# Second attention: beta's addition on VectorE, scatter tails set by halves of a round

## The chip, the core and the metric

The kernel runs on one core of a Trainium2 chip. The metric is the device time of one execution in microseconds (us). PE is TensorE, DVE VectorE, ACT ScalarE, POOL GpSimd, SP SyncE. TensorE's clock has two levels, 1.2 and 2.4 GHz; the profile gives the granted clock as a share of the full one.

## The reference

Four layers act on x, 4096 tokens (64 sequences of 64) of 256 floats, all in float32; each adds its result to x.

```python
x = x + xattn0(layernorm(x), ctx)       # attention over the channel axis, 8 heads
x = x + ffn0(layernorm(x))              # 16 experts, the best 2 per token, and a shared expert
x = x + xattn1(layernorm(x), ctx)       # below
x = x + ffn1(layernorm(x))              # 32 experts, the best 4 per token

# the end of xattn1: ctx_h are the heads' results
delta = rs * (ctx_h @ Wo.T + bo)
delta = (delta - mean(delta)) / sqrt(var(delta) + 1e-5) * ln_gamma + ln_beta

# ffn1, as ffn0 in its routing
logits = x @ gate_w.T + gate_b
top, idx = top_k(logits, 4); weight = softmax(top)
y = sum over the 4 of weight * expert[idx](x)
```

## The kernel before

All 32 tiles of x (128 tokens x 256) stay in SBUF. The stages follow each other, each written as one list of steps per engine; each engine runs its list in order and waits on semaphores. Eight groups of four tiles (`GT = 4`, `NG = 8`) are routed. Stages: the first attention (to about 785 us), the shared expert with the first routing (788 to 905), the first experts (to 1060), the second attention with the second routing (1060 to 1440), the second experts (to 1710), and a last stage that sums and stores.

**Routing.** For a group, VectorE picks the best K experts of each token (`choose`), PE counts ranks (`make_ranks`), VectorE turns them into row numbers in a DRAM tensor `rows_in` (`place_rows`, semaphore `slots_ready`) and writes weights (`weigh`, or ScalarE's sigmoids in the shared expert). GpSimd then sends the group's rows in K rounds (`scatter`): round k writes the normalised row of each token to its k-th expert's place, with four indirect DMAs, one per tile. A row is 272 floats: 256 of the token and a tail of 16, whose first two are `DEST` (where the expert's result for this token and k belongs in `by_token`) and `WEIGHT`. GpSimd copies these two into the tail before each round, which needs the DMAs of the group's round before to have read the row. `tails_set` counts the rounds whose tails are set. K is 2 in the first routing, 4 in the second, 32 rounds there.

**Second attention.** Step r of each engine's list works on several tiles at once (j = r % 4, g = r // 4). VectorE, in order: `choose` for group g-2 (j = 0), the norm of group g+2 (j = 3), `clip` of r+1 (L1862), statistics, `place_rows` and `weigh` for g-2 (j = 1), `residual` of r-2 (L1897, L1900), `normalise` of r (L1869, L1872), `delta_statistics` of r-1 (L1880 to L1889). Residual: `scaled = (delta - mean) * gamma`, then `x = scaled * rstd + xb`, where `xb = x + beta` comes from GpSimd (`add_beta`, L1975). PE in step r: `values`, `scores` of r+1 (L1650), transposes, `context_transposes` of r-1 (L1668; waits for VectorE's heads and delta), keys or queries, `outputs` of r (L1679), `projection` of r-1 (L1687), logits of g-1 (L1071, j = 3), ranks of g-2 (j = 0). GpSimd in step r: `delta_deviation` of r-2 (L1981, the power -1/2 that the residual needs), `add_beta` of r-1, a round of scatters from r = 10 on, the power for a group's norm (L1456). Before r = 4 or so it also adds the first experts' results to x (`add_parts`, L1964 and L1967). The 32 rounds go one per step in a fixed list; after the first 22 come, by group and k, (5,2), (6,0), (5,3), (6,1), (7,0), (6,2), (7,1), (6,3), (7,2), (7,3). The last six need the last group's routing or follow it.

**SP's queue at the end of this stage.** 16 pieces of 0.5 MB of the next experts' weights `w_gu` go into a region the attention used (L1609). Each waits for a value of `tails_set`, so that they are spread over the last rounds:

```python
for n, (into, source) in enumerate(later):
    sp.wait_ge(rt.tails_set, len(in_order) + 1 + n * (len(rounds) - len(in_order) - 2) // len(later))
    sp.dma_start(into, source).then_inc(later_written, 16)
```

With 22 in order and 32 in all, piece n waits for 23 + n // 2. Behind them on SP, `table_pads` writes a block of 128 zero rows behind each expert's last row, 16 on SP's queue and 16 on ScalarE's, four row numbers loaded (L722) and then four DMAs (L726), and then the experts' block loads begin (L863). The experts read each block's `DEST` and `WEIGHT` with ScalarE and store the weighted results with indirect DMAs on GpSimd.

## Time and profile before

| | |
|---|---|
| median of 3 runs | 1776.12 us (1773.91 to 1784.85) |
| profiled execution | 1775.95 us, of which 1774.0 between first and last instruction |
| mean granted TensorE clock | 0.944 |
| busy, share of the span | PE 86%, DVE 75%, ACT 62%, POOL 62% |
| DMA moved | 167.66 MB, mean 95 GB/s |

Busy shares are means over stages with different limits. A row of the order of time reads: start, duration, engine, line, operation, output and input, shape, and in brackets how long the engine stood idle before it and what ended that. In the chain of waits each row is the start and length of a piece of the chain that ended last. "remote" is a semaphore whose setter the profile did not identify. L numbers are lines of the kernel before.

### The profile page before, as it was taken

What the parts mean: (1) busy time and instruction counts of PE and PEld (TensorE: products, weight loads), DVE (VectorE), ACT (ScalarE), POOL (GpSimd) and SP (SyncE); (2) the same over time, 40 slices, a digit from 0 to 9 for tenths busy, and PEclk for the clock granted to TensorE, in tenths of its full rate; (3) what the DMA queues carried; (4) which work ended last, traced back from release to release, by engine and by line L of the source; (5) the groups of instructions that cost most, each with busy time, mean ns of one, the idle gap of its engine ahead of it and who ended that gap; (6) DMA issues with size and microseconds to landing.
All of it is one profiled execution on the core that took longest, in us unless ns stands there. A gap on an engine that the chain in (4) does not pass through costs nothing.

```text
span 1774.0 us, 43982 instructions
## 1 busy us (share of the span) xinstructions
PE 1533.0 (86%) x14968; PEld 1236.6 (70%) x14968; DVE 1332.5 (75%) x2901; ACT 1094.1 (62%) x3516; POOL 1093.0 (62%) x1111
## 2 busy tenths in 40 slices
PE   6999999999999999989967755998895179999966
PEld 5888888888888888866646642565564179998955
DVE  6889899899999989876634344798886248887876
ACT  5888888888888888843335433656551056666610
POOL 4767667676666667647635554647776636666642
PEclk9999999999999999989989986999995589999988
DMA  8400000000000000022255424112213855554456
GB/s 230 128 20 20 20 20 20 20 20 20 12 19 20 20 20 20 8 97 84 79 176 155 151 80 161 49 38 94 83 71 113 311 167 165 162 158 150 125 200 275
DMA packets 103082, 167.66 MB, mean 95 GB/s; under 512 B 20224, under 2 KB 75981, under 8 KB 102481
## 3 DMA queue, kind: packets, MB, share of 16 engines
q1 hardware_dynamic: 73984, 103.46, 19.1%
q0 software_dynamic: 22272, 56.15, 8.6%
q10 hardware_dynamic: 6608, 5.25, 1.0%
q8 instruction: 124, 2.03, 0.5%
q14 instruction: 94, 0.76, 0.2%
HBM read 95.31 MB, written 75.76 MB: 96 GB/s over the span
## 4 chain that ended last, share of the span: by engine, by line
PE 68%; DVE 11%; issue 9%; POOL 3%; another core or an unknown queue 3%; ACT 2%; ACTq 1%; DMA 1%; SPq 1%; DVEq 0%; POOLq 0%
PE layers_banks L323 13%; PE layers_banks L294 13%; PE layers_banks L309 9%; PE layers_banks L890 9%; PE layers_banks L901 5%; PE layers_banks L1269 3%; PE layers_banks L277 3%; PE layers_banks L283 3%; PE layers_banks L878 2%; DVE weights L1862 2%; PE layers_banks L1282 1%; PE layers_banks L2152 1%; POOL l_rows_in L1179 1%; PE layers_banks L1071 1%
## 5 line engine op out<-in xcount | busy, mean ns | idle before, releaser
L468 POOL TENSOR_TENSOR w_down<-w_down,layers_arena 128x1024 f32<-128x1024 f32 x256 | 483.5, 1894 | 230.3 <-DVE layers_arena L424 229.3
L389 ACT ACTIVATE w_down<-layers_banks,layers_arena 128x256 f32<-128x256 f32 x1024 | 468.7, 498 | 2.8 <-DVE layers_arena L418 2.8
L1010 POOL DMA_INDIRECT l_by_token<-layers_arena x240 | 245.0, 1021 | 192.3 <-issue 104.2
L429 DVE COPY w_down<-layers_banks 128x1024 f32<-128x1024 f32 x256 | 312.2, 1220 | 40.4 <-PE layers_banks L309 36.2
L418 DVE TENSOR_REDUCE layers_arena<-layers_banks 128x4 f32<-128x1024 f32 x256 | 309.4, 1209 | 29.4 <-PE layers_banks L294 29.3
L294 PE MATMUL layers_banks<-layers_arena 64*128 64x256 f32 x2048 | 277.9, 383 | 3.7 <-ACT w_down L389 2.2
L323 PE MATMUL layers_banks<-w_down,layers_arena 128*64 128x256 f32 x2048 | 249.4, 385 | 1.7 <-DVE w_down L429 1.3
L389 ACT ACTIVATION_READ_ACCUMULATOR w_down<-layers_banks,layers_arena 128x1 f32 x1024 | 238.0, 232 | 0.0
L890 PE MATMUL layers_banks<-layers_arena 128*128 128x128 f32 x1600 | 204.1, 280 | 34.3 <-ACT layers_arena L933 30.7
L1179 POOL DMA_INDIRECT l_rows_in<-layers_arena,l_routing_group_slots x192 | 190.3, 991 | 57.7 <-issue 44.7
L309 PEld LDWEIGHTS layers_banks<-ident,w_down 64*128 64x128 f32 x4096 | 168.4, 138 | 77.5 <-issue 71.6
L890 PEld LDWEIGHTS layers_banks<-layers_arena 128*128 128x128 f32 x1600 | 192.3, 195 | 40.4 <-issue 40.0
L294 PEld LDWEIGHTS layers_banks<-layers_arena 64*128 64x128 f32 x2048 | 208.7, 188 | 6.0 <-issue 5.5
L309 PE MATMUL layers_banks<-ident,w_down 64*128 64x64 f32 x4096 | 178.7, 224 | 17.4 <-DVE w_down L429 3.4
L323 PEld LDWEIGHTS layers_banks<-w_down,layers_arena 128*64 128x64 f32 x2048 | 142.1, 136 | 61.5 <-DVE w_down L429 1.5
L986 DVE TENSOR_SCALAR layers_arena<-layers_banks,layers_arena 128x256 f32<-128x256 f32 x240 | 104.5, 477 | 75.5 <-PE layers_banks L901 41.0
L924 ACT ACTIVATE layers_arena<-layers_banks 128x512 f32<-128x512 f32 x120 | 70.5, 587 | 92.8 <-PE layers_banks L878 78.2
L353 ACT ACTIVATE layers_arena<-layers_banks 128x512 f32<-128x512 f32 x128 | 75.8, 592 | 82.0 <-PE layers_banks L283 82.0
L933 ACT ACTIVATE layers_arena<-weights 128x512 f32 (+1 forms) x240 | 119.6, 547 | 3.7 <-issue 3.7
L957 DVE TENSOR_SCALAR layers_arena<-layers_banks,l_block_bias 128x128 f32<-128x128 f32 x160 | 48.8, 346 | 87.1 <-PE layers_banks L890 84.7
L878 PE MATMUL layers_banks<-ident,layers_arena 128*128 128x128 f32 x480 | 75.4, 281 | 44.0 <-DMA layers_arena<-l_rows_in 44.0
L878 PEld LDWEIGHTS layers_banks<-ident,layers_arena 128*128 128x128 f32 x480 | 61.9, 146 | 57.0 <-issue 44.1
(227 smaller groups left out, 2552.3 us busy)
## 6 DMA issues: line engine op xcount, KB each, us to landing
layers_arena<-l_rows_in SPq DMA_DIRECT2D x240, 136.0 KB
weights<-l_by_token SPq DMA_DIRECT2D x32, 512.0 KB, 9.7
layers_arena<-in_ctx SPq DMA_DIRECT2D x64, 128.0 KB, 2.7
layers_arena<-l_by_token SPq DMA_DIRECT2D x32, 256.0 KB, 2.7
weights<-in_w_gu SPq DMA_DIRECT2D x16, 512.0 KB
l_rows_in<-zeros SPq DMA_DIRECT2D x1, 4352.0 KB
x_sb<-in_x SPq DMA_DIRECT2D x32, 128.0 KB, 2.5
w_down<-in_w_down SPq DMA_DIRECT2D x1, 4096.0 KB
```

The source lines that it names most:

```text
L294: last = nc.tensor.matmul(ps_s[:, b, 2 * h + qt, :], q_sb[half, p % 2, b, qt * P:(qt + 1) * P], ctx_d[half, p // TILE % 2, b, :], start=Tr ...
L309: last = nc.tensor.transpose(ps_t[:, d, kt, c * S:(c + 1) * S], prob[half, n % 4, c, kt * P:(kt + 1) * P], ident[half, half])
L323: last = nc.tensor.matmul(ps_qo[b * S:(b + 1) * S, 0, 0:A_N], vb[:, p // TILE % 2, kt, b, head * S:(head + 1) * S], prob_t[:, p % 2, b, kt ...
L389: last = nc.scalar.activation(prob[:, n % 4, c, :], ps_s[:, n % 2, c, :], ACT.Exp, bias=negmax[:, n % 2, c:c + 1], accum_out=sums[:, n % 2 ...
L418: nc.vector.tensor_reduce(negmax[:, n % 2, :], ps_s[:, n % 2, :, :], AX.X, ALU.max, negate=True).then_inc(max_ready, 1)
L429: nc.vector.tensor_copy(prob_t[:, n // 2 % 2, n % 2, :, :, :].rearrange("p k c (d s) -> p d (k c) s", d=2), ps_t[:, :, :, :].rearrange("p ...
L468: nc.gpsimd.tensor_tensor(prob[:, n % 4, :, :], prob[:, n % 4, :, :], rsum[:, n % 2, :].unsqueeze(2).to_broadcast([P, 4, A_N]), ALU.mult). ...
L878: last = nc.tensor.transpose(ps_x[:, q % 2, b, kt, :], rows[:, q % BODY, b, kt * P:(kt + 1) * P], sb["ident"][:, :])
L890: last = nc.tensor.matmul(ps_gu[:, q % 2, u, b, :], w_now[:, q % 2, b, kt, u * P:(u + 1) * P], rows_t[:, q % 2, b, kt, :], start=(kt == 0) ...
L933: last = nc.scalar.activation(w_now[:, r % 2, b, :, :].rearrange("p k n -> p (k n)"), w_gu[:, bass.ds(e[b], 1), :, :].rearrange("p a k n - ...
L1010: pool.indirect_dma_start(m.by_token, bass.IndirectOffsetOnAxis(ap=place, axis=0), outs[:, r % OUTS, b, :], None, bounds_check=T * m.K - 1 ...
L1179: pool.indirect_dma_start(m.rows_in, bass.IndirectOffsetOnAxis(ap=self.slots[:, slot, n:n + 1], axis=0), xn[:, j, :], None).then_inc(self. ...
```

## The change

`add_beta` leaves GpSimd; VectorE does the same addition at the start of `residual`, ahead of the waits for the power and for `scaled`, and the wait for `xb_ready` now stands before the last instruction. `place` (integers) and `weight` (floats) become one float tensor `tails` with the two side by side; one copy sets both numbers. A round is cut into halves of two tiles, each with its copy, its wait on `tails_set`, its two DMAs and a semaphore of its own, `scattered[slot][half]`, so the copy for a half waits only for the DMAs of the same half of the round before. `tails_set` counts halves, and the values on which SP's weight pieces wait are rewritten. ScalarE turns `DEST` into an integer when it copies it in the experts.

```diff
-        self.place = sbt("_place", [P, NG, K, GT], I32)
-        self.weight = sbt("_weight", [P, NG, K, GT], F32)
+        self.tails = sbt("_tails", [P, NG, K, GT, 2], F32)
...
                 nc.scalar.activation(dest[:, q % TAILS, :].bitcast(I32),
-                                     rows[:, q % BODY, :, DEST].bitcast(I32), ACT.Copy)
+                                     rows[:, q % BODY, :, DEST], ACT.Copy)
...
-        self.scattered = [ph.sem(f"scattered{n}") for n in range(Routing.RING)]
+        self.scattered = [[ph.sem(f"scattered{n}_{half}") for half in range(2)] for n in range(Routing.RING)]
...
     def scatter(self, pool, it, q, xn, k, turn, done):
-        sent = 16 * GT
+        sent = 16 * (GT // 2)
         slot, lap = (it * 2 + q) % self.RING, (it * 2 + q) // self.RING
         if k == 0:
             done(pool, self.slots_ready, it, q)
             done(pool, self.weights_ready, it, q)
-        else:
-            pool.wait_ge(self.scattered[slot], lap * sent * m.K + sent * k)
-        nc.gpsimd.tensor_copy(xn[:, :, DEST].bitcast(I32), m.place[:, it * 2 + q, k, :])
-        nc.gpsimd.tensor_copy(xn[:, :, WEIGHT], m.weight[:, it * 2 + q, k, :]).then_inc(self.tails_set, 1)
-        pool.wait_ge(self.tails_set, turn + 1)
-        for j in range(GT):
-            n = j * m.K + k
-            pool.indirect_dma_start(m.rows_in, bass.IndirectOffsetOnAxis(ap=self.slots[:, slot, n:n + 1], axis=0),
-                                    xn[:, j, :], None).then_inc(self.scattered[slot], 16)
+        for half in range(2):
+            tiles = slice(half * GT // 2, (half + 1) * GT // 2)
+            if k > 0:
+                pool.wait_ge(self.scattered[slot][half], lap * sent * m.K + sent * k)
+            nc.gpsimd.tensor_copy(xn[:, tiles, DEST:WEIGHT + 1], m.tails[:, it * 2 + q, k, tiles, :]).then_inc(self.tails_set, 1)
+            pool.wait_ge(self.tails_set, 2 * turn + half + 1)
+            for j in range(half * GT // 2, (half + 1) * GT // 2):
+                n = j * m.K + k
+                pool.indirect_dma_start(m.rows_in, bass.IndirectOffsetOnAxis(ap=self.slots[:, slot, n:n + 1], axis=0),
+                                        xn[:, j, :], None).then_inc(self.scattered[slot][half], 16)
...
-            sp.wait_ge(rt.tails_set, len(in_order) + 1 + n * (len(rounds) - len(in_order) - 2) // len(later))
+            sp.wait_ge(rt.tails_set, 2 * len(in_order) + 2 + 2 * n * (len(rounds) - len(in_order) - 2) // len(later))
...
         def residual(it, r):
+            tdone(dve, x_ready, it, r - 1)
+            nc.vector.tensor_tensor(xb[:, r % 2, :], tile, w["beta"][:, :], ALU.add).then_inc(xb_ready, 1)
             tdone(dve, rstd_d_ready, it, r)
-            tdone(dve, xb_ready, it, r)
-            tdone(dve, x_ready, it, r - 1)
             nc.vector.scalar_tensor_tensor(out=scaled[:, :], ...).then_inc(scaled_ready, 1)
             tdone(dve, scaled_ready, it, r)
+            tdone(dve, xb_ready, it, r)
             nc.vector.scalar_tensor_tensor(out=tile, ...).then_inc(x_ready, 1)
...
-        def add_beta(it, r):
-            tdone(pool, scaled_ready, it, r - 2)
-            tdone(pool, x_ready, it, r - 2)
-            nc.gpsimd.tensor_tensor(xb[:, r % 2, :], x_sb[...], w["beta"][:, :], ALU.add).then_inc(xb_ready, 1)
...
-            if texists(it, r - 1):
-                add_beta(it, r - 1)
```

`mark_sent` waits for both halves; `weigh`, the sigmoids of the shared expert and the last stage write or read `tails[..., 1]` instead of `weight`; the iotas of the places and of the zero rows' `DEST` make floats.

## Rows read from the trace of the kernel before

**Rows 1.** Busy time by stretch (us; instructions), PEclk, DMA share, GB/s
```profile
core 0: us, PE busy (x) PEld busy (x) DVE busy (x) ACT busy (x) POOL busy (x), PEclk, DMA share, GB/s
788.00:905.00 117.00, 107.99 (x543) 70.86 (x541) 71.40 (x325) 40.95 (x70) 74.20 (x102) 0.99 0.27 101
1226.00:1259.00 33.00, 29.73 (x301) 19.80 (x301) 28.95 (x96) 19.45 (x33) 24.61 (x34) 1.00 0.26 85
1390.00:1415.00 25.00, 1.43 (x4) 1.03 (x4) 2.25 (x8) 0.00 (x0) 18.89 (x27) 0.50 1.04 383
```

**Rows 2.** Chain of waits, end of the shared expert: start, us, what
```profile
906.16 1.77 DMA l_rows_in<-zeros
```

**Rows 3.** Order of time, GpSimd then VectorE, end of part A
```profile
1141.08 0.55 POOL L1981 TENSOR_TENSOR layers_arena<-layers_arena,minus_half 128x1 f32<-128x1 f32 x1
1141.60 0.73 POOL L1975 TENSOR_TENSOR layers_arena<-x_sb,w_beta 128x256 f32<-128x256 f32 x1
...
1141.67 0.94 DVE L1897 SCALAR_TENSOR_TENSOR layers_arena<-layers_arena,w_gamma 128x256 f32<-128x256 f32 x1 [2.81 <-POOL layers_arena L1981]
```

**Rows 4.** Waits of VectorE, 1143 to 1349 us: total, times, longest
```profile
DVE weights L1862 <- remote: 4.9, 3, 2.4
DVE layers_arena L1082 <- remote: 3.6, 2, 1.8
DVE weights L1862 <- PE layers_banks L1650: 1.4, 1, 1.4
...
DVE layers_arena L1465 <- POOL layers_arena L1456: 0.3, 2, 0.2
```

**Rows 5.** Order of time, GpSimd, last rounds of scatters
```profile
1387.27 0.19 POOL L1174 COPY layers_arena<-l_place 128x4 int32<-128x4 int32 x1 [1.70 <-DVE l_weight L1126]
...
1416.89 0.19 POOL L1174 COPY layers_arena<-l_place 128x4 int32<-128x4 int32 x1 [2.58 <-DMA l_rows_in<-layers_arena,l_routing_group_slots]
...
1417.48 0.98 POOL L1179 DMA_INDIRECT l_rows_in<-layers_arena,l_routing_group_slots  x1 [0.28 <-POOL layers_arena L1175]
1418.77 0.96 POOL L1179 DMA_INDIRECT l_rows_in<-layers_arena,l_routing_group_slots  x1 [0.30 <-issue]
...
1421.29 0.96 POOL L1179 DMA_INDIRECT l_rows_in<-layers_arena,l_routing_group_slots  x1 [0.30 <-issue]
```

**Rows 6.** Chain of waits over SP's queue, end of the attention
```profile
1404.28 0.93 SPq L1609
...
1407.07 0.36 SPq L726
...
1408.72 0.69 SPq L726
...
1418.96 0.33 SPq L726
...
1419.48 0.33 SPq L726
...
1423.26 1.93 DMA l_rows_in<-zeros
```

**Rows 7.** GpSimd's groups by line, 1050 to 1440 us
```profile
L1975 POOL TENSOR_TENSOR layers_arena<-x_sb,w_beta 128x256 f32<-128x256 f32 x32 | 23.9, 747 | 0.0
...
L1174 POOL COPY layers_arena<-l_place 128x4 int32<-128x4 int32 x32 | 8.4, 261 | 14.1 <-DMA l_rows_in<-layers_arena,l_routing_group_slots 12.3 <-DVE l_weight L1126 1.7
```

**Rows 8.** VectorE's groups by line, 1143 to 1349 us
```profile
L1897 DVE SCALAR_TENSOR_TENSOR layers_arena<-layers_arena,w_gamma 128x256 f32<-128x256 f32 x25 | 12.2, 486 | 0.3 <-issue 0.3
```

**Rows 9.** Order of time, VectorE, inside part B
```profile
1221.80 0.47 DVE L1897 SCALAR_TENSOR_TENSOR layers_arena<-layers_arena,w_gamma 128x256 f32<-128x256 f32 x1
...
1226.65 0.29 DVE L1082 TENSOR_TENSOR layers_arena<-layers_banks,w_gate_b 128x128 f32<-128x128 f32 x1 [1.76 <-remote]
```

**Rows 10.** Order of time, VectorE, start of the attention
```profile
1068.55 0.42 DVE L1848 TENSOR_TENSOR x_sb<-x_sb,layers_arena 128x256 f32<-128x256 f32 x1
1068.89 0.42 DVE L1846 TENSOR_TENSOR layers_arena<-layers_arena 128x256 f32<-128x256 f32 x1
```

**Rows 11.** Chain of waits in part B, PE's last piece
```profile
1320.47 1.72 PE layers_banks L1071 x16
```

More of the change, by code:

```diff
@@ L1125, in weigh @@
         dve.sem_inc(self.passed, 1)
-        nc.vector.tensor_tensor(m.weight[:, bass.ds(it * 2 + q, 1), :, :].rearrange("p a k j -> p (a j) k"), self.powers[:, :, :],
+        nc.vector.tensor_tensor(m.tails[:, it * 2 + q, :, :, 1].rearrange("p k j -> p j k"), self.powers[:, :, :],
                                 self.share[:, 1, :].unsqueeze(2).to_broadcast([P, GT, m.K]), ALU.mult)\
@@ L1186, in mark_sent @@
     def mark_sent(self, pool, it, q):
-        n = 16 * GT * self.m.K
+        n = 16 * (GT // 2) * self.m.K
         slot, lap = (it * 2 + q) % self.RING, (it * 2 + q) // self.RING
-        pool.wait_ge(self.scattered[slot], n * (lap + 1))
+        for half in range(2):
+            pool.wait_ge(self.scattered[slot][half], n * (lap + 1))
         pool.sem_inc(self.rows_sent, 1)
@@ L1335, in sigmoids @@
             done(act, rt.behind_ready, it, q)
-            nc.scalar.activation(m.weight[:, bass.ds(it * 2 + q, 1), 0, :], rt.behind[:, :, 1].unsqueeze(1), ACT.Sigmoid,
+            nc.scalar.activation(m.tails[:, it * 2 + q, 0, :, 1], rt.behind[:, :, 1], ACT.Sigmoid,
                                  scale=-1.0)
-            nc.scalar.activation(m.weight[:, bass.ds(it * 2 + q, 1), 1, :], rt.behind[:, :, 1].unsqueeze(1), ACT.Sigmoid)\
+            nc.scalar.activation(m.tails[:, it * 2 + q, 1, :, 1], rt.behind[:, :, 1], ACT.Sigmoid)\
                 .then_inc(rt.weights_ready, 1)
@@ L2180, in expert_weights @@
             nc.vector.tensor_tensor(weighted[:, :, :, :], onehot[:, :, :, :],
-                                    m.weight[:, g, :, :].rearrange("p k j -> p j k").unsqueeze(3)
+                                    m.tails[:, g, :, :, 1].rearrange("p k j -> p j k").unsqueeze(3)
                                     .to_broadcast([P, GT, K, E]), ALU.mult).then_inc(expert_steps, 1)
```

10 lines of the change are left out of this document (4 added, 6 removed).

## Prediction

> **What bounds the kernel now.** I first read the table of stretches [rows 1]. The change touches the two stages that scatter rows: the shared expert of the first layer (788 to 905 us) and the second attention with its tail (1060 to 1440 us). In the first, PE is busy for 108.0 of 117 us at granted clock 0.99 and GpSimd for 74.2: PE sets the pace, and GpSimd's waits cost nothing. The chain of waits ends the stage on the zero rows that ScalarE's queue writes, which land 1.77 us after 906.16 [rows 2], while GpSimd's last scatter is out before 904. The rest of the execution contains none of the edited steps but a weight copy, a table setup and a strided read.
>
> The second attention has four parts, read from the table of stretches and the chain of waits.
> A, up to about 1142 us: GpSimd adds the expert rows back to back, with the beta additions between them, and VectorE waits for its powers, 2.81 us before L1897 at 1141.67 [rows 3].
> B, 1143 to 1349 us: VectorE is busy for 28.95 of 33 us in a group of four tiles, GpSimd for 24.61, PE for 29.73, at full clock [rows 1]. The chain of waits lies mostly on VectorE. What VectorE still waits for is PE: 4.9 + 1.4 us before the clip (L1862), 3.6 us before the logits are read (L1082), 9.9 us in all; for GpSimd it waits 0.3 us [rows 4]. Those called remote are semaphores that PE sets: the two lines wait for PE alone or for ScalarE, which was waiting too.
> C, 1355 to 1369 us: a serial run of VectorE steps, with the last two residuals in it, leads to the last group's scores.
> D, from 1387.27 us: GpSimd issues the last six rounds, 24 indirect DMAs, while SP sends the last pieces of w_gu and then writes 16 blocks of zero rows. GpSimd's last issue starts at 1421.29 and takes 0.96 us [rows 5], SP's last zero rows are issued up to 1423.26 and land 1.93 us later, and only then are the blocks loaded [rows 6]. The two queues end within about a microsecond.
>
> **The change part by part.** The terms are worked out against the profiled execution: 1775.95 us, 1774.0 of it span, 0.17 us under the median of the three runs, which I neglect.
>
> The addition on GpSimd: 32 instructions of 747 ns, 23.9 us, go from its queue [rows 7]. In B and D they delay nothing that VectorE waits for longer than 0.3 us [rows 4]. In A two of them stand in GpSimd's unbroken run before the power at 1141.08 that VectorE waits for; one like that at 1141.60 takes 0.73 us [rows 3], of which some 0.7 count, as the next one starts a little before the end: together 1.4 us. That at 1141.60 runs beside L1897, which takes 0.94 us there and 0.47 us at 1221.80 [rows 3, 9]: another 0.5 us. Term A is -1.9 us. What is late next there is VectorE itself; as it waited 2.81 us and the new addition runs inside the wait, nothing is taken back.
>
> The same addition on VectorE: the nearest row is L1848 and L1846, the same 128x256 addition of floats from SBUF: 0.42 us each, and the next independent one starts 0.34 us after its start [rows 10]. I take 0.34 us, as the instruction behind (L1897) does not depend on it; 0.42 is the upper end. It is put ahead of both waits, so it can also run while VectorE would stand still. B has 25 of the 32 residuals [rows 8], 8.5 us. From it goes what falls under the waits for PE. The waits before L1082 (about 1.8 us) come after a stretch in which PE runs without VectorE for two steps: two additions, 0.68 us, vanish in each of the two. The chain of waits runs over PE alone from 1309 to the end of L1071, which starts at 1320.47 [rows 11]: two more. The three remote waits and the other before the clip each have one addition since PE last waited for VectorE (for the mask of the group, L1108), 0.34 us each. Together 3.4 us. I also count the 0.3 us of waits for GpSimd as saved, and round: term B is +5.0 us, between -3.0 (PE's waits of 9.9 us could swallow all 8.5 and shrink further, if it is GpSimd's load that delays PE's semaphores) and +10.5 (25 x 0.42, nothing hidden). C takes two more, in a serial run, +0.7 us (at most 0.84). The stall before L1897 at 1349.51, which GpSimd's queue causes, gets shorter, but the next VectorE step waits for PE's projection anyway: 0.
>
> The copy by halves: before, a round takes 0.59 us from the first of two copies to the first DMA, then 1.29 us to the second, 2.52 to the fourth and 0.96 for that, 5.36 us in all [rows 5]. After, each half is one copy; the second of the two starts some 0.12 us behind the first, so one copy takes about 0.47 us to its first DMA, then 1.29 and 0.96 us: 2.72 us, a round 5.44 us. So a copy more in the middle costs what the merging saves, within 0.1 us a round. The semaphore per half takes the wait before a round's copy: such waits sum to 12.3 us [rows 7], of which 2.58 us stand before the last round, at 1416.89 [rows 5]. GpSimd would end its last issue about 2.3 us earlier. In B that leaves GpSimd waiting for VectorE instead. In D the zero rows hide it. In the shared expert PE hides it: 0. If PE did not, that stage has 14.5 us of such waits, but its end is ScalarE's queue, not GpSimd's.
>
> The queue moved past: SP's w_gu pieces wait on the same counter. Before, piece n waited for round 22 + n//2 (counted from 0); after, for half round 45 + n: even pieces come one half later, odd ones with the first half of the next round. The last piece was released by the copy of the 30th round and issued at 1404.28, right behind its neighbour [rows 6]; now it waits for the first half of the 31st, four rounds of 5.44 us after 1387.27, that is at 1409.2. Behind it in SP's queue stand the loads of 16 row numbers and the 16 zero blocks, whose first was issued at 1407.07, 2.8 us after the last piece: it moves to about 1411.6, 2.4 us after the release as only one piece is in front, +4.5 us. Who waits for these blocks: every block load of the experts. Against that stands their pace. Before, most of the first eight took 0.69 us each to issue, behind the pieces in the same queue; the last eight 0.33 us, 0.52 us apart [rows 6], 3.3 us for four with their row numbers. With one piece in front instead of two, 2.7 us apart, I take 3.3 us per four: the last leaves 11.6 us after the first, at 1423.2, where it left before. Bounds: -0.5 us (if the loads of row numbers are quicker too) and +5.4 us (pace as before, and 0.1 us per round). I take +0.7 us, term D, nearer to the lower end because the pieces then come out one by one: 0.5 MB and two scatters of 0.14 MB in 2.72 us are 295 GB/s, under the 383 GB/s of the stretch 1390 to 1415 [rows 1].
>
> ScalarE's dest copy now converts instead of copying bits, the iotas make floats, and the weights are read and written at a step of two: 4 to 16 numbers per partition each, on engines that are not late; 0, at most 0.3 us.
>
> Sum: -1.9 + 5.0 + 0.7 + 0.7 = +4.5 us, 1780.5 us.
>
> A rule speaks against the move. The rows first: L1897, which reads two tensors, took 0.94 us beside a GpSimd addition and 0.47 us beside an indirect DMA [rows 3, 9]. The Trainium skill says (SBUF — State Buffer, SBUF: two separate sides) that a VectorE instruction with two SBUF inputs and a GpSimd instruction that reads SBUF exclude each other for their whole length. By that rule each of the 32 additions can hold a copy or a power on GpSimd, or wait for one; it is the fourth case below.
>
> **The rivals.**
> 1. Faster: GpSimd, not VectorE, sets the pace of B. For it: the remote wait that ends at 1226.65 [rows 9] ends 0.9 us after GpSimd's last issue of a round, and the other four of these waits 0.9 to 1.2 us after such an issue. Against: 0.3 us of waits for GpSimd. If the relief takes PE's waits away, B gives -2 us, A -1.9, D -0.5, C -0.7 (its stalls too): -5 us, 1771 us.
> 2. Slower by SP's tail: the zero blocks keep the old pace, as the pieces have only moved with them. Decided by whether the first eight go out 0.70 us apart: +5.4 for D instead of +0.7, 1785 us.
> 3. Slower by VectorE: the additions are paid in full, as PE's waits move with VectorE (PE itself waits for heads and delta). B is then +8.5 to +10.5: 1784 to 1786 us. With case 2 as well 1791 us, and 1794 and over 1% slower if PE's clock, full through B, also falls to half for a few us because PE stands still more, as in the stretch 1390 to 1415.
> 4. The two engines exclude each other: an addition that meets a copy (0.19 us) or power on GpSimd waits for it. In B each of 25 would pay at least 0.19 us: +4.8 us on the sum, 1785 us. L1897 at its usual place is not stretched beside an indirect DMA (0.47 us at 1221.80 [rows 9]), so only copies and powers can collide.
>
> **How the numbers follow.** Forecast 0.58, with its own range 1776 to 1785; case 1 0.17; case 2 0.10; case 3 0.10, a third of it with case 2; case 4 0.05. All but the join of 2 and 3, and half of the tail of case 1, lie between 1770 and 1789, which is the range. About 1% (18 us) is what a measurement of this kernel tells from no change: faster by that 0.03 (case 1 with much more of it than 5 us), slower 0.05 (the join, and more than I know of in B), within it 0.92.
>
> **What would show it.** A: L1897 near 1141 starts about 1.5 us earlier and takes 0.5 us. B: a new row of 32 additions of 0.42 us on VectorE, VectorE busy about 1 us more in a 33 us stretch, waits before L1082 shorter by 0.7 us, none for GpSimd; GpSimd's copies wait for DMAs for under 4 us in all. D: the last w_gu piece 22 us after the last group's first copy, the zero blocks 0.52 us apart. I am wrong if a group takes the same time with the additions in it (case 1), if the blocks stay at 0.70 us (case 2), or if L1082 waits as long as before (case 3).

## The result and the profile after

The changed kernel took 1811.03 us (median of 4 runs, 1808.15 to 1813.98), the kernel before 1775.17 us in the same series: a ratio of 1.0174, 95% interval 1.0145 to 1.0204. It is slower by 1.7%, 36 us. The forecast was 1780.5 us, in a range of 1770 to 1789.

The profiled execution has a span of 1812.0 us, 38.0 more than before. I put each VectorE instruction of one trace beside the same one of the other. The table gives the time between fixed marks: start of the routing in the shared expert, its table of rows, the first sum of the attention, the residuals (L1897) of tiles 8 and 28, the first and the last clip of the second experts (L957), and VectorE's last instruction.

| us | shared expert | first experts | to residual 8 (A) | residual 8 to 28 (most of B) | to the first clip (C, D) | second experts | last stage |
|---|---|---|---|---|---|---|---|
| before | 116.3 | 157.6 | 119.1 | 161.5 | 92.8 | 257.5 | 68.6 |
| after | 129.3 | 156.4 | 115.8 | 177.9 | 95.3 | 267.4 | 68.0 |
| difference | +13.0 | -1.2 | -3.3 | +16.4 | +2.5 | +9.9 | -0.6 |

So the shared expert, which I had costed at 0, lost 13 us, B lost 16.4 instead of 5, and the second experts, where almost nothing was edited, 10.

The table of stretches of the kernel after, for the same stages as [rows 1]: the first is 13 us longer, the second starts 13 us later (columns as there):

```profile
788.00:918.00 130.00, 114.26 (x545) 73.61 (x544) 70.94 (x325) 41.01 (x70) 76.49 (x102) 0.94 0.25 92
1239.00:1272.00 33.00, 27.62 (x264) 17.69 (x264) 27.22 (x87) 18.85 (x31) 19.28 (x27) 0.95 0.21 75
```

No engine is fuller. In B all of them have less to do in 33 us (PE 27.6, before 29.7; VectorE 27.2, before 29.0; GpSimd 19.3, before 24.6): the time went into waiting. In the shared expert PE stands still for 15.7 us instead of 9.0, and is busy for 6.3 us more with the same work, as its granted clock is 0.94 instead of 0.99. VectorE's waits of the kernel after in B, 1187 to 1370 us, show for whom (total, times, longest; L1870 is L1869 of before, the reciprocal that follows PE's outputs, L1863 the clip), to be read against [rows 4]:

```profile
DVE layers_arena L1870 <- remote: 13.9, 10, 3.0
DVE weights L1863 <- PE layers_banks L1651: 5.4, 6, 1.8
DVE layers_arena L1081 <- remote: 1.4, 2, 0.7
DVE layers_arena L1870 <- PE layers_banks L1680: 1.2, 1, 1.2
```

In the shared expert of the kernel after, such a wait stands where there was none. The order of time, GpSimd, then PE, then VectorE:

```profile
832.36 0.98 POOL L1179 DMA_INDIRECT l_rows_in<-layers_arena,l_routing_group_slots  x1 [0.28 <-issue]
833.65 0.96 POOL L1179 DMA_INDIRECT l_rows_in<-layers_arena,l_routing_group_slots  x1 [0.31 <-issue]
...
831.82 1.46 PE L1283 MATMUL layers_banks<-weights,layers_arena 128*128 128x256 f32 x6
...
836.75 1.52 PE L1270 MATMUL layers_banks<-layers_arena,weights 128*128 128x512 f32 x3 [3.13 <-DVE x_sb L1394]
...
834.27 0.88 DVE L1394 SCALAR_TENSOR_TENSOR x_sb<-layers_banks,layers_arena,x_sb 128x256 f32<-128x256 f32 x2 [2.36 <-remote]
835.73 0.88 DVE L1394 SCALAR_TENSOR_TENSOR x_sb<-layers_banks,layers_arena,x_sb 128x256 f32<-128x256 f32 x2 [0.58 <-remote]
```

PE's last product of L1283 ends at 833.28; its semaphore is recorded at 835.71, and L1394, which adds the product to x, starts its second pair at 835.73, 1.1 us after GpSimd's last indirect DMA (834.61). PE, which needs L1394, stands still for 3.13 us. GpSimd issued eight such DMAs from 824.10 on with nothing but 0.20 us copies between them. Before, it stood for 1.68 us in the middle of the eight, waiting for the first four to land:

```profile
830.76 0.19 POOL L1174 COPY layers_arena<-weights 128x4 int32<-128x4 int32 x1 [1.68 <-DMA l_rows_in<-layers_arena,l_routing_group_slots]
```

The same stall comes at 853.25 (2.98 us), and there PE's granted clock falls too, to 0.50 from 852.4 to 859.2 us: L1270 x16 takes 10.08 us from 853.25 on, where it took 7.10 us from 836.75 on at 1.00.

**When PE's semaphores come.** The trace also records when each semaphore was raised. I matched every product of PE that raises one with the next record of it, in part B of twelve traces (before, after and the first ten experiments on the whole kernel), and call it held when it comes over 0.35 us behind the product's end. Some records are missing and count as held, so these are rough counts.

```
product ends                         semaphores   held
during 1st DMA of an unbroken run        317       29%
during 2nd                               226       52%
during 3rd                               260       80%
during 4th                               158       85%
0 to 0.4 us after the run                 68       96%
0.4 to 0.8 us after                       77       32%
0.8 to 1.2 us after                       60        7%
later, or no run near                    800        0%
```

The held ones come in bunches, two fifths of them 0.7 to 1.1 us after the end of an issue, most others inside the run. This is my theory 1: an unbroken run of indirect DMAs on GpSimd (nothing between them, or only the 0.20 us copies) holds PE's semaphores back. The change lengthened the runs (shared expert) and moved their start (attention).

### The profile page after: what moved, and what is told of

Read it like the earlier page. It is cut to its first block, busy times and chain, and to the rows that moved or that the text cites. A ratio compares the mean times of both kernels' runs of the same rounds, so it can differ in the third digit from the quotient of the medians.

```text
span 1812.0 us, 43952 instructions
## 1 busy us (share of the span) xinstructions
PE 1554.5 (86%) x14968; PEld 1249.0 (69%) x14968; DVE 1340.5 (74%) x2933; ACT 1098.7 (61%) x3516; POOL 1071.2 (59%) x1079
## 4 chain that ended last, share of the span: by engine, by line
PE 68%; DVE 9%; issue 8%; POOL 5%; another core or an unknown queue 3%; ACT 2%; ACTq 1%; DMA 1%; SPq 1%; DVEq 0%; POOLq 0%
PE layers_banks L323 13%; PE layers_banks L294 12%; PE layers_banks L309 8%; PE layers_banks L889 8%; PE layers_banks L900 4%; PE layers_banks L1270 3%; PE layers_banks L277 3%; PE layers_banks L283 3%; PE layers_banks L877 3%; POOL l_by_token L1009 2%; POOL l_rows_in L1179 2%; PE layers_banks L1630 2%; PE layers_banks L2146 1%; PE layers_banks L1070 1%
## 5 line engine op out<-in xcount | busy, mean ns | idle before, releaser
L1009 POOL DMA_INDIRECT l_by_token<-layers_arena x240 | 240.8, 1003 | 211.2 <-DVE layers_arena L985 117.7
L889 PE MATMUL layers_banks<-layers_arena 128*128 128x128 f32 x1600 | 209.6, 284 | 34.3 <-ACT layers_arena L932 26.7
L889 PEld LDWEIGHTS layers_banks<-layers_arena 128*128 128x128 f32 x1600 | 196.6, 199 | 42.3 <-issue 41.9
```

Of the source, the lines that this page charges most:

```text
L889: last = nc.tensor.matmul(ps_gu[:, q % 2, u, b, :], w_now[:, q % 2, b, kt, u * P:(u + 1) * P], rows_t[:, q % 2, b, kt, :], start=(kt == 0) ...
L1009: pool.indirect_dma_start(m.by_token, bass.IndirectOffsetOnAxis(ap=place, axis=0), outs[:, r % OUTS, b, :], None, bounds_check=T * m.K - 1 ...
```

## The experiments

The ratio is always to the kernel before in the same series; its median was 1769 to 1780 us in these series. The times of stages are each from the one traced execution of a kernel, and B stands for residual 8 to 28. The first four take the change apart.

**e1_beta_only**: the kernel before with the addition moved (the diff of `residual`, `add_beta` and its call). 

> The kernel before with beta's addition on VectorE and nothing else of the change. Theory 1 (semaphores that PE sets reach the waiting engines about 1 us after GpSimd's last indirect DMA of an unbroken run; the halves made the runs longer, the addition did not): shared expert unchanged (first block load near 908.7 us), part A 3 to 4 us shorter, part B within -2 to +5 us, in all 1771 to 1779 us. Theory 2 (VectorE's additions cost what part B lost, 18 us): 1788 to 1794 us.

Measured: 1792.92 us, 1.0078 [1.0051, 1.0106]. Shared expert 119.0, B 175.7 us (+14.2).

**e2_halves_only**: the kernel after with `add_beta` back on GpSimd. 

> The kernel after with beta's addition back on GpSimd: only the tails as floats, the copy per half and the semaphore per half are left of the change. Theory 1: the shared expert keeps its +13 us and part B most of its +18 us, 1798 to 1812 us. Theory 2: only the shared expert's +13 us stay, 1785 to 1790 us.

Measured: 1789.98 us, 1.0068 [1.0045, 1.0091]. Shared expert 130.4 (+14.1), B 159.3 us (-2.2).

**e3_round_wait**: the kernel after, with

```diff
-            if k > 0:
-                pool.wait_ge(self.scattered[slot][half], lap * sent * m.K + sent * k)
+            if k > 0 and half == 0:
+                for both in range(2):
+                    pool.wait_ge(self.scattered[slot][both], lap * sent * m.K + sent * k)
```

> The kernel after, but the first half of a round waits for the DMAs of both halves of the group's round before, so GpSimd pauses between two rounds of a group as it did in the kernel before; copies, floats, addition on VectorE stay. Theory 1: the remote waits of the shared expert go and its +13 us with them, part B is within 0 to +6 us of before: 1772 to 1783 us. Theory 2 (the additions): 1790 to 1796 us. Theory 3 (the second copy in the middle of a round, or two semaphores, cost it): about 1810 us.

Measured: 1790.43 us, 1.0068 [1.0039, 1.0097]. Shared expert 115.9, B 173.1 us.

**e4_shared_round_wait**: the same wait in the shared expert's second round alone. 

> The kernel after with that wait for the whole round in the shared expert alone; the second attention is that of the kernel after. Theory 1: 11 to 14 us less than after, 1797 to 1800 us, with first block loads near 909 us. Theory 3: no gain, about 1811 us. If the long alternation in the second experts stage (10 us) is set off by the phase in which this stage is entered, it may come or go here: then 1787 us.

Measured: 1793.51 us, 1.0086 [1.0057, 1.0114]. Shared expert 118.3, B 177.4 us.

What follows: the two losses have two causes. The shared expert's comes with the halves (e2) and goes with the wait (e3, e4: -13 and -11 us), whatever the copies and semaphores are, so theory 3 (the second copy) falls. B's comes with the moved addition alone: my expectation for e1 was wrong, and so were that for e2, where I had B lose by the halves, and that for e3 in B (+11.6 us, where I had 0 to 6). The totals of e1, e2 and e3 lie in the ranges that I had named for theory 2, that the additions themselves cost it; e4's, 1793.51 us, lies under the range of theory 1. But 14 us for 20 residuals are 0.7 us each, and an addition takes 0.42. In e1 VectorE's remote waits stand before the reciprocal (14.6 us in B), and PE is busy in B for only 1.5 us more than before, so its clock is not what B lost there. The order of time of e1 in one step (PE, then GpSimd, VectorE, ScalarE):

```profile
1266.27 1.13 PE L1679 MATMUL layers_banks<-layers_arena,weights 128*64 128x34 f32 x32
...
1265.68 1.05 POOL L1179 DMA_INDIRECT l_rows_in<-layers_arena,l_routing_group_slots  x1 [0.29 <-POOL layers_arena L1175]
...
1269.61 0.96 POOL L1179 DMA_INDIRECT l_rows_in<-layers_arena,l_routing_group_slots  x1 [0.30 <-issue]
...
1271.45 0.26 DVE L1869 RECIPROCAL layers_arena<-layers_banks 128x16 f32<-128x16 f32 x1 [3.73 <-remote]
...
1271.73 0.38 ACT L1763 ACTIVATE layers_arena<-layers_banks 64x256 f32<-64x256 f32 x1 [2.93 <-PE layers_banks L1622]
```

L1679 ended at 1267.40; its semaphore is recorded at 1271.43, 4.03 us later, and those of the next three pieces of PE (L1687, L1071, L1622, ended at 1268.45, 1270.16 and 1271.10) at 1271.48, 1271.64 and 1271.70: one bunch, 0.86 us after the run's end. In the kernel before, the same step had the addition on GpSimd at 1252.74, its run began at 1254.23 and L1679 had ended at 1253.62, just ahead of it; the reciprocal (1255.73) did not wait:

```profile
1252.49 1.13 PE L1679 MATMUL layers_banks<-layers_arena,weights 128*64 128x34 f32 x32
...
1252.74 0.87 POOL L1975 TENSOR_TENSOR layers_arena<-x_sb,w_beta 128x256 f32<-128x256 f32 x1
...
1254.23 1.05 POOL L1179 DMA_INDIRECT l_rows_in<-layers_arena,l_routing_group_slots  x1 [0.29 <-POOL layers_arena L1175]
...
1255.73 0.25 DVE L1869 RECIPROCAL layers_arena<-layers_banks 128x16 f32<-128x16 f32 x1
```

So theory 1b: GpSimd's addition was a spacer that kept the run behind PE's outputs.

**e5_power_for_beta** puts a spacer back where the addition was:

```diff
+        def spare_power(it, r):
+            tdone(pool, scaled_ready, it, r - 2)
+            tdone(pool, x_ready, it, r - 2)
+            pool.wait_ge(spare_made, 2 * r)
+            nc.gpsimd.tensor_tensor(spare[:, 0:1], sb["onesf"][:, :], sb["minus_half"][:, :], ALU.pow).then_inc(spare_made, 1)
+            nc.gpsimd.tensor_copy(spare[:, 1:2], sb["onesf"][:, :]).then_inc(spare_made, 1)
```

> Beta's addition on VectorE, and in its old place in GpSimd's list a power of one column (0.57 us) and a copy (0.19 us) into spare numbers, with the waits that the addition had: GpSimd is as busy before each round of scatters as in the kernel before, VectorE as busy as in the kernel after. Theory 1b (taking the addition off GpSimd lets its run of four indirect DMAs start some 0.8 us sooner, so that the semaphore of PE's outputs falls into the run and comes about 1 us behind its end): most of the 14 us that part B lost with beta's addition on VectorE alone come back, residual 8 to residual 28 in 162 to 168 us (161.5 before, 175.7 with the addition moved), 1778 to 1784 us. Theory 2 (VectorE's addition costs it): 174 to 178 us there, 1792 us or more.

Measured: 1775.75 us, 1.0035 [1.0014, 1.0056]. B 165.8 us: with idle work on GpSimd, 10 of the 14 us are back.

**e6_beta_left_out**: no addition on either engine. 

> Beta is not added anywhere (left out of the computation): neither engine has the addition, all else is the kernel before. Theory 1b: part B is slower than before although both engines have less to do, residual 8 to 28 in 168 to 174 us, in all 1782 to 1790 us. Theory 2: as before or a little faster, 158 to 162 us there, 1770 to 1776 us.

Measured: 1776.22 us, 1.0036 [1.0006, 1.0066]. B 170.4 us (+8.9): less work on both engines, and slower. VectorE's remote waits of e6 in B:

```profile
DVE layers_arena L1869 <- remote: 16.7, 11, 2.5
DVE layers_arena L1082 <- remote: 2.5, 3, 1.2
```

The four kernels make a square for B: addition on GpSimd 161.5, on neither 170.4, on VectorE with the spacer 165.8, on VectorE alone 175.7. VectorE's addition costs 4.3 to 5.3 us, the missing spacer 8.9 to 9.9.

**e7_beta_gated**: e1 and a wait for PE's outputs ahead of the round.

```diff
                 q, k = rounds[r - FIRST]
+                if texists(it, r):
+                    tdone(pool, pv_made, it, r)
```

> Beta's addition on VectorE, copies and semaphores as in the kernel before, and one wait more on GpSimd: the round of step r starts only after PE's outputs of step r (L1679). The wait holds one round back by 1 to 3 us, GpSimd has the room. Theory 1b: VectorE's remote waits before L1869 (14.6 us in part B with the addition moved) fall under 4 us, residual 8 to 28 in 160 to 167 us, in all 1774 to 1782 us. Theory 2: no gain on the addition moved alone, 1793 us; if the held rounds push the last ones back, more than that.

Measured: 1774.09 us, 1.0026 [1.0, 1.0052]. B 167.1 us; no remote wait before the reciprocal is left in it, but VectorE waits 6.9 us for the powers of a group's norm (L1456), which stand behind the held round.

**e8_gated_beta_dve** moves those powers ahead of the round, **e9_gated_beta_pool** does the same with the addition on GpSimd, **e10_after_mended** with the whole change and e3's wait.

> The addition on VectorE, copies and semaphores as before, GpSimd's round waits for PE's outputs of its step, and the powers of a group's norm now stand ahead of the round, where they waited behind it in the run with the gate alone (VectorE waited 6.9 us for them in part B). Theory 1b: those 6.9 us go, residual 8 to 28 in 158 to 163 us (161.5 before, 167.2 with the gate alone); against the kernel before -6 to 0 us. If the powers then hold GpSimd back because VectorE's statistics come later than PE's outputs, rounds are late and it is +2 to +8 us.

> The same gate and order of GpSimd's powers, but beta's addition stays on GpSimd: the kernel before and the gate alone. GpSimd has 0.75 us more per step and rounds start later, so its queue sets the pace more often: residual 8 to 28 in 163 to 170 us, +2 to +8 us against the kernel before. If the gate by itself is what matters and not who adds, it is the same as the run with the addition on VectorE within 3 us.

> The kernel after (addition on VectorE, floats, copy per half, SP's thresholds in halves) with both mends: the first half of a round waits for the whole round before, and the attention's rounds wait for PE's outputs, powers ahead. If held semaphores explain all of the 35 us, this is within -6 to +6 us of the kernel before; what is left above the run without halves is the price of the halves and of SP's thresholds, at most 3 us. If the change has another cost: +12 us or more.

Measured: 1784.33, 1790.26 and 1782.68 us, ratios 1.0082 [1.0065, 1.0099], 1.0126 [1.0109, 1.0144] and 1.0077 [1.006, 1.0094]; B 175.7, 179.6 and 174.9 us. This is the second outcome that I had named for e8, but larger than its +2 to +8 us, and e9 is outside all that I had named: ahead of the round GpSimd waits for the variances of the norm (34.0 us in B of e8), and the power for the next residual comes late. e10 lands where I had put another cost of the change, but e8 and e9, which have no halves, are as slow, so these three say nothing about the halves; e11 was made for that.

**e11_after_gate_wait**: the whole change with e3's wait and e7's gate. 

> The kernel after, whole (addition on VectorE, floats, copy per half, SP's thresholds), with the wait for the whole round before and with the round held until PE's outputs of its step; the powers stay behind the round. If held semaphores explain the loss: shared expert within 4 us of before, residual 8 to 28 in 165 to 170 us as in the run with the gate alone (167.2), in all +2 to +8 us against the kernel before, of +35 before mending. If halves or thresholds have a cost of their own: +12 us or more.

Measured: 1785.89 us, 1.0035 [1.0004, 1.0066]. Shared expert 115.7, B 168.3 us. Of 1.7% one fifth is left (by the interval, between nothing much and two fifths). The change still stands in the code, but the wait takes away what the semaphore per half was for.

**e12_before_gate**: the kernel before with the gate. 

> The kernel before with the gate alone; beta's addition stays on GpSimd, ahead of the round. If the gate only undoes what the moved addition did, it has little to mend here and holds rounds back: residual 8 to 28 in 162 to 168 us, +1 to +6 us against the kernel before. If PE's late semaphores (8.5 us of VectorE's waits in part B before) are mended by it: 155 to 160 us, -2 to -6 us.

Measured: 1787.55 us, 1.0030 [1.0006, 1.0055]. B 164.3 us, 2.8 more than before: with the addition on GpSimd the gate gains nothing.

**e13_power_between**: e7 with the powers of the norm between the second and the third DMA of a round. 

> Addition on VectorE, copies and semaphores of before, gate; the power of a group's norm stands between the second and the third DMA of its round instead of behind the fourth. Of the 6.9 us that VectorE waited for these powers in part B with the gate alone, 2.5 us each in four steps, nearly all should go: residual 8 to 28 in 160 to 165 us (161.5 before, 167.2 gate alone), -3 to +2 us against the kernel before. If the broken run matters too (semaphores delivered at the break), a little less still; if the run's end moves on to the next product instead, 166 us or more.

Measured: 1785.51 us, 1.0028 [1.0006, 1.0051]. B 167.0 us, no gain. The waits for these powers are gone, but remote waits before the clip are up to 8.0 us from 3.5. I read this as the case that I had named last, the run's end moved on to the next of PE's semaphores; GpSimd's own wait for the norm's variances in the middle of four rounds (15.2 us in B) stretches the round too, and no run tells the two apart.

**e14_beta_between** and **e15_beta_powers_between** break the run without a new wait:

```diff
         for j in range(GT):
+            if j == 2 and between is not None:
+                between()
             n = j * m.K + k
...
-                rt.scatter(pool, it, q, xf[:, q % XF, :, :], k, r - FIRST, gdone)
+                rt.scatter(pool, it, q, xf[:, q % XF, :, :], k, r - FIRST, gdone,
+                           (lambda: add_beta(it, r - 1)) if texists(it, r - 1) else None)
```

> The kernel before; beta's addition stays on GpSimd but stands between the second and the third indirect DMA of the round (0.75 us) instead of ahead of the round. The run of four becomes two of two; the first starts 0.75 us sooner, as when the addition was moved away. If the length of the run counts: fewer PE semaphores held, residual 8 to 28 in 156 to 162 us (161.5 before), -5 to 0 us against the kernel before. If only the place of the run's start and end counts: as with beta left out, 166 to 171 us, +3 to +8 us.

> The same, and the power of a group's norm stands there too in its two of four steps (1.05 us more of a break). If length counts: another 0 to 3 us less than with the addition alone, unless the power waits for VectorE there. If place counts: within 3 us of it.

Measured: e14 1766.21 us, 0.9977 [0.9951, 1.0002], B 157.7 us; e15 1770.74 us, 1.0002 [0.9977, 1.0027], B 160.6 us. VectorE's waits of e14 from 1187 to 1345 us, which reach 8 us beyond its B, have no remote one left, and none stands earlier in B either:

```profile
DVE layers_arena L1899 <- POOL layers_arena L1983: 7.6, 5, 2.2
DVE layers_arena L1467 <- POOL layers_arena L1458: 2.4, 3, 0.8
DVE layers_arena L1899 <- issue: 0.3, 1, 0.3
```

Length counts, not only place: in e14 the run starts as early as in e6, and B is 12.7 us shorter. Counted as in the table above, 66 of PE's 134 semaphores in B are held in e6, 48 in the kernel before, 29 of 135 in e14. The break also puts the second pair of DMAs back to where it was before, so length and place are not wholly apart. What VectorE waits for now is GpSimd's power. e15, where I had expected up to 3 us less again, took 2.9 us more in B: it has no remote wait either, but 6.6 us of waits for the residual's power. e14 is the fastest kernel of the study, though its interval just takes in no change.

**The effect by itself.** Three small kernels leave out the whole computation. m1_semaphores_alone: 

> None of the computation: PE and VectorE hand a semaphore to and fro (a 128x128 product, a copy out of PSUM), 24 turns in each of six phases, while GpSimd does nothing, issues 16 indirect DMAs of 128 rows of 272 floats in runs of 2, 4, 8 and 16 with a wait for their landing between, or makes 24 additions of 128x256. Then ScalarE and VectorE do the same. Theory 1: turns are even (about 1 us or less) when GpSimd is idle or adds; beside the runs a turn is stretched to the rest of the run plus about 1 us, so the longest wait is 2 to 3, 4 to 6, 8 to 11 us for runs of 2, 4 and 8. If the run does not hold semaphores back, turns are even throughout and theory 1 falls; if only PE's are held, ScalarE's turns stay even.

Measured: even turns of 1.18 us in every phase with PE, 0.60 to 0.68 us with ScalarE, beside runs of 16 DMAs too. By this the theory falls, or needs more from PE than one product in 1.18 us.

m2_semaphores_busy: 

> None of the computation: PE makes bursts of 1, 8 or 32 products of 128x34 and raises a semaphore at the end of each, VectorE answers each with a copy, PE may be one burst ahead; GpSimd stands still, issues 16 indirect DMAs in runs of 4 with a wait for their landing between, or in one run of 16, or (with bursts of 32) makes 24 additions. In the kernels, PE's semaphores were late only within 1.2 us of such a DMA, and not in the first measurement of this kind, where PE made one product in 1.2 us. If it takes both, many instructions of PE and a run: turns are even with bursts of 1 whatever GpSimd does, even with bursts of 32 when it stands still or adds, and with bursts of 32 beside a run single turns are 2 to 5 us longer, ending about 1 us behind the run. If turns are even in all phases, something else of the kernels is needed, and the part that PE's load plays stays open.

Measured: a product took 0.43 us here (all go to one place), so PE had fewer instructions than in the attention. Turns are even (3.41 us with bursts of 8, 13.65 with 32) but for the runs of 16. Beside one of those, started at 260.11, VectorE's copies come at 262.72, 266.13, 269.55, then 277.78 and 282.81: 4.8 us late, from its eleventh DMA on. I had expected runs of 4 to do it.

m3_semaphores_fast spreads the products over 16 places and halves their width, so that PE runs more of them:

```diff
-                            last = nc.tensor.matmul(bank[:, turn % 2, 0:34], left[:, :], right[:, 0:34], start=True, stop=True)
+                            half, place = slice(c % 2 * 64, c % 2 * 64 + 64), c // 2 % 8 * 64
+                            last = nc.tensor.matmul(bank[half, turn % 2, place:place + 34], left[:, 0:64], right[:, 0:34],
+                                                    start=True, stop=True)
```

> As the second measurement of semaphores, but PE's 32 products of a burst go to 16 different places, as in the attention, so that they run at some 0.04 us each instead of 0.43: a turn should take 1.2 to 1.6 us. Phases: GpSimd still, runs of 4, 8 and 16 indirect DMAs, 24 additions. If PE's rate is what matters, runs of 4 now stretch turns by 2 us or more, runs of 8 and 16 by 3 to 8 us, the still and the adding phase not at all. If only the length of the run matters: even turns beside runs of 4, as before.

Measured: a turn takes 1.87 us when GpSimd stands still (32 products and their weights, 0.06 us each). The turn that meets the first run of 4 takes 6.83 us, at a granted clock of 1.00 until 86.4 us. From 86.4 to 113.7 us, and again from 151.3 us on, the granted clock is 0.50, and there an even turn takes 3.41 us: against that stand the 5.67, 6.35 and 5.66 us of the turns beside the other runs of 4, 14.56 us beside the second run of 8 and 15.17 us in the run of 16. The turn that meets the first run of 8, mostly at full clock, takes 8.16 us. 24 additions leave the turns at 3.41 us. VectorE's copies in m3 when GpSimd stands still, from the first run of 4 on, which starts at 81.26, and at the lower clock with GpSimd still:

```profile
42.84 0.19 DVE L2291 COPY got<-layers_banks 128x34 f32<-128x34 f32 x1 [1.67 <-PE layers_banks L2282]
44.71 0.19 DVE L2291 COPY got<-layers_banks 128x34 f32<-128x34 f32 x1 [1.67 <-PE layers_banks L2282]
...
87.00 0.19 DVE L2291 COPY got<-layers_banks 128x34 f32<-128x34 f32 x1 [6.63 <-remote]
89.14 0.19 DVE L2291 COPY got<-layers_banks 128x34 f32<-128x34 f32 x1 [1.95 <-PE layers_banks L2282]
94.81 0.19 DVE L2291 COPY got<-layers_banks 128x34 f32<-128x34 f32 x1 [5.47 <-PE layers_banks L2282]
101.16 0.19 DVE L2291 COPY got<-layers_banks 128x34 f32<-128x34 f32 x1 [6.16 <-remote]
...
177.92 0.19 DVE L2291 COPY got<-layers_banks 128x34 f32<-128x34 f32 x1 [3.22 <-PE layers_banks L2282]
```

The semaphore of the burst that ends at 82.53 is recorded at 86.97, 0.77 us behind the run's last issue. But PE itself is slowed in that run too, which the attention did not show:

```profile
80.47 2.43 PE L2282 MATMUL layers_banks<-right,left 128*64 128x34 f32 x70 [0.34 <-POOLq L2255]
83.29 0.42 PE L2282 MATMUL layers_banks<-right,left 128*64 128x34 f32 x6 [0.38 <-issue]
84.02 0.36 PE L2282 MATMUL layers_banks<-right,left 128*64 128x34 f32 x5 [0.31 <-issue]
```

After 70 products it goes on in small groups with 0.3 to 0.4 us between them until the run is over. Then its clock drops: the granted clock is 1.00 from 36 to 86.4 us and 0.50 from there to 113.7 us. The turn that ends with the copy at 94.81 is long because PE's own last product ends at 94.77; its semaphore comes at once. So the effect of a run stands with nothing else of the kernel around, in two forms, late semaphores and late products. It takes both sides: with one product in 1.18 us a run of 16 does nothing, with one in 0.43 us only a run of 16 does something, late in it, and with some 17 per us a run of four is enough. Where between these it sets in was not measured.

Could the late semaphores be PE's work still going on, since its ends are modelled? It is not an artefact of how the ends are shown: in m3 the copies come every 1.87 us beside a still GpSimd and 6.83 us apart beside a run, and in the kernels 800 semaphores away from runs came on time. Nor did PE stand still meanwhile in e1's step: it began L1687, L1071 and L1622 at 1267.32, 1268.29 and 1269.99, with the semaphore of L1679 still out. The Trainium skill (Perfetto Trace Analysis, Tensor Engine Instruction) says that the end shown for a product is an estimate and that its semaphore is raised once PSUM has confirmed the writes; that is why I timed the waiting engines and not PE's rows. Whether in the attention only the semaphore is late, or already the writes that it tells of, no run shows.

## Why the prediction was wrong

**The step that failed** is "The semaphore per half takes the wait before a round's copy", with "In the shared expert PE hides it: 0", and beside it "32 instructions of 747 ns, 23.9 us, go from its queue [...]. In B and D they delay nothing that VectorE waits for longer than 0.3 us". Both took idle or unneeded time on GpSimd as worth nothing. It was what kept its indirect DMAs apart, or away from PE's outputs. The experiments put 11 to 13 us on the first (after against e3, e4) and 9 to 10 us on the second (the square). Of 36 us this is some 60%. In the shared expert about half of it is the lower clock that follows the stalls; in the sum the clock had no term, only a place in rival 3. I had the sign in front of me: rival 1 notes that five remote waits end 0.9 to 1.2 us after GpSimd's last issue of a round. I took that as GpSimd's load, which the change would relieve; it was the run's length and place.

**VectorE's addition** (+5.0 us in B, for 25 residuals) was sized about right: 4.3 to 5.3 us for the 20 between the marks, by the square of e1, e5, e6 and before. L1896 takes 0.42 us each in B, the upper end of what I had taken. 20 of those are 8.4 us, so a part did run inside VectorE's waits, as I had it; whether inside those that I had listed was not followed.

**Rival 3** (additions paid in full, B +8.5 to +10.5) has the right place and the wrong price, and **rival 1** the right suspect with the wrong sign. **Rival 4** fails in B, where I had priced it: in e1, whose copies are those of before, the two copies of a round take 0.23 and 0.22 us there (before 0.29 and 0.18), the residual's power 0.58 us (before 0.57) and VectorE's addition 0.42 us at most. In A it does show, beside GpSimd's additions of expert rows: in the kernel after two of VectorE's additions take 0.69 us instead of 0.42, and the power at 1142.37 takes 0.74 us instead of 0.55. This agrees with the rule of the Trainium skill that I had weighed (SBUF — State Buffer, SBUF: two separate sides), but it is under a microsecond in all.

**Term A** (-1.9 us) came out at -3.3 us. VectorE's rows there, of the kernel after, as [rows 3]:

```profile
1148.11 0.69 DVE L1896 TENSOR_TENSOR layers_arena<-x_sb,w_beta 128x256 f32<-128x256 f32 x1
1150.40 0.48 DVE L1898 SCALAR_TENSOR_TENSOR layers_arena<-layers_arena,w_gamma 128x256 f32<-128x256 f32 x1 [1.60 <-POOL layers_arena L1977]
```

L1898 takes 0.48 us instead of 0.94, the wait before it is 1.60 instead of 2.81 us. The other traces give A 115.8 to 121.3 us, e1 with the addition moved 120.3, so nothing of its size is sure, nor its sign.

**Term D** (+0.7 us): from the first copy of the last six rounds to the landing of the last zero rows it took 37.92 us before and 40.07 after (1413.23 to 1453.30), +2.1. The chain of waits of the kernel after, as [rows 6]:

```profile
1435.49 0.33 SPq L1610
...
1436.56 0.33 SPq L725
...
1451.53 1.77 DMA l_rows_in<-zeros
```

The last piece leaves 22.3 us after that copy, where I had 22. The first zero rows follow after 1.07 us instead of 2.4, but the blocks then take 14.5 us instead of 11.6: the pace of [rows 6] held for longer (rival 2 in part), and the two errors cancel in part.

**The second experts** (+9.9 us) are not explained by a term. Pairs of blocks there take 6.4 or 7.2 us. In the second pattern GpSimd issues four DMAs without a pause and then waits 2.3 us for VectorE; in the first, pairs stand 0.8 us apart. GpSimd of the kernel after, a stretch in which the first turns into the second:

```profile
1504.91 0.98 POOL L1009 DMA_INDIRECT l_by_token<-layers_arena  x1 [1.11 <-issue]
1506.20 1.08 POOL L1009 DMA_INDIRECT l_by_token<-layers_arena  x1 [0.30 <-issue]
1508.07 0.98 POOL L1009 DMA_INDIRECT l_by_token<-layers_arena  x1 [0.79 <-issue]
1509.36 0.98 POOL L1009 DMA_INDIRECT l_by_token<-layers_arena  x1 [0.30 <-issue]
1510.68 0.98 POOL L1009 DMA_INDIRECT l_by_token<-layers_arena  x1 [0.33 <-issue]
1511.96 0.99 POOL L1009 DMA_INDIRECT l_by_token<-layers_arena  x1 [0.30 <-issue]
1515.26 0.98 POOL L1009 DMA_INDIRECT l_by_token<-layers_arena  x1 [2.31 <-DVE layers_arena L985]
```

Some 12 or 13 pairs in a row of the kernel after run so, and 12 of e3; before, e2, e5 and e7 have at most three in a row. The stage took 254 to 258 us in ten of seventeen traces, 262 to 270 in the rest, e12 with this stage and its inputs unchanged among them. The traced execution of e3 took 1798.57 us, its median is 1790.43, so the second pattern need not be in most executions. Of PE's 234 semaphores in this stage 108 are held in the kernel after and 96 before, by the count above, so it may be the same effect, locked in by chance of phase; no run tested that. Whether the change makes the pattern likelier is open, and so is about a quarter of the loss.

## What to carry to other kernels

Before you take work or a wait away from the engine that issues indirect DMAs, look at what it keeps apart: list the unbroken runs of issues, before and after, and which semaphores of PE fall into them. Where PE is busy with many small products, break such runs with work that the engine has to do anyway rather than saving it, and try the break alone first. A "remote" wait that ends a fixed time after another engine's burst is a price with an owner, not noise; cost it with both signs.

## What the hardware showed

An unbroken run of indirect DMAs on GpSimd holds back PE's semaphores: in m3, with 32 products in a 1.87 us turn, four DMAs stretched a turn to 6.8 us; at the lower clock, where the turn is 3.41 us, four stretched it to 5.7 to 6.4 us and eight to 14.6 us. In the first such run PE's own products came in groups of 5 or 6 with 0.3 to 0.4 us between. GpSimd's additions did nothing of the kind, and ScalarE's turns stayed at 0.60 to 0.68 us beside runs of 16. With one product in 1.18 us PE had no late turn either. What in the chip the two share was not found. No run issued these DMAs from another engine, so whether it is the issue on GpSimd or the traffic of the rows is open too. The medians over all executions go with the traced stages: e1's ratio is 14 us where its B grew by 14.2, e14's -4 us where B shrank by 3.8. An addition of 0.75 to 0.96 us in the middle of a run of four was enough to take all of VectorE's remote waits from part B (e14).
